# A mixture-of-experts decoder block on one core: router rows scattered without their weights, the weights sent after them in narrow scatters, the router cut into three parts

## The chip, the cores and the metric

One Trainium2 chip, one of its cores. The engines are named as in the profile: PE is TensorE (matmuls, PEld its weight loads), DVE VectorE, ACT ScalarE, POOL GpSimd, SP the SyncE queue that only issues transfers. The metric is the device time of one execution in microseconds; a kernel's time is the median of its runs.

## The reference, cut to what matters

1024 tokens (4 sequences of 256) of width 256 go through three blocks, each followed by a residual sum and a layer norm without gain: causal attention with 16 heads, a mixture in which a token's expert comes from its id, and a mixture of four experts of width 1024 with a learned router. The change touches the third block's router:

```python
logits = x @ Wr + br                       # 4 logits for each token
probs = jax.nn.softmax(logits, axis=-1)
top_w, top_idx = jax.lax.top_k(probs, 1)   # one expert, and its probability
...
h = jax.nn.silu(g) * u
y = jnp.einsum('tef,efd->ted', h, Wd)
sel = jnp.take_along_axis(y, top_idx[:, :, None], axis=1)[:, 0]
out = sel * top_w                          # then x = layernorm(x + out)
```

## The kernel before, in words

Everything is written out by hand: each engine has its own program in program order, and every dependence is a semaphore (`wait_ge`, `then_inc`). A helper `link` makes the next instruction of the same engine wait for the one before.

The **second block** leaves its rows in `XS`, 11 tiles (NS) of 128 rows; a row holds 256 values, the token's number (a large number in an empty row) and one place for the weight. It is a software pipeline of 17 rounds (`for s in range(NS + LOGIT_LAG)`, one such loop on PE, ACT and DVE). In round s tile s is transposed (L1614), tile s-1 goes through gate and product (L1155), the transposed product of tile s-2 is split into a high and a low half (L746, L1174), tile s-3 gets its residual and its statistics (L1187, L1196, L1198), tile s-4 is normalised (L1192), tile s-5 is transposed for the router (L1691, copied at L764), and tile s-6 gets its four logits (L1682). Between L1198 and L1192 POOL works out the inverse deviation of the tile (`inv_std2`, L545 and L546: add, then power).

The **router** sorts rows by expert. It runs in parts (PARTS: tiles 0 to 5, then 6 to 10). For a part DVE adds the bias, takes the largest logit and subtracts it (`logits`, L865 to L869), makes the one-hot row (`top_expert`, L877 to L883), PE counts with two matmuls how many rows of each expert stand in the same tile and ahead of a row (`count`), ACT takes the exponentials (`exps_router`), DVE forms the weight, one over their sum, and writes it into the row (`top_weight`), and DVE turns counts into a place for every row (`places`, L901 to L911). The first part's work is put into rounds 12 and 13 of DVE's loop, the second part's behind the loop. `slot_tiles` and `tile_rows` then give each of the 11 tiles of the third block its expert and its first row (L837 to L919).

POOL issues, behind the inverse deviation of the last tile, one indirect DMA for each tile that scatters its 128 rows to their places in the HBM buffer `sorted3` (L554), and then a small memset (L563) on which DVE waits before it splits three more weight chunks (L831, WINDOW). PE warms its clock with 16 matmuls of no use (`keep_warm`) when the last places are out, waits for all scatters, warms with 6 more, waits for the weight splits (`c_lo`, GATES) and transposes the first tile (L1720). SP waits for all scatters and loads the 11 tiles back in sorted order (L421).

The **third block** runs over these 11 tiles. PE does gate and up products for half a tile at a time (L1735 to L1737) and the product down (L1752 to L1754), which for tile 0 comes behind the gates of tile 2; DVE and ACT gate and split between them and also split the last weight chunks. DVE scales the result of a tile with the row's weight and adds the residual (`statistics`, L1240), POOL works out the inverse deviation, DVE normalises (L1252), and POOL scatters the rows to the output (L571).

Of the kernel before, what the change touches and what calls it, by code (L numbers as in the profile page):

```python
# [16 lines left out]
P = 128  # L17
# [33 lines left out]
PARTS = ((0, 6), (6, NS))  # L51
PART_BANK = (6, 7)
# [15 lines left out]
def build(nc, x_tok, xT, ids, wqkvT, woT, ctxT, Wr, br, Wf, out):  # L68
    ctx = ExitStack()
    with ctx:  # L70
# [24 lines left out]
        region = sb("region", [P, E], F32)  # L95
# [118 lines left out]
        sorted3 = nc.dram_tensor("sorted3", [NR3, ROW], F32, kind="Internal").ap()  # L214

# [20 lines left out]
        scat2, scat3 = sem("scat2"), sem("scat3")  # L236
# [108 lines left out]

        block = ctx.enter_context(nc.Block())
# [3 lines left out]
        def _(sp):  # L350
# [43 lines left out]
            for step in range(STEPS):  # L394
# [30 lines left out]
        def _(pool):  # L425
# [3 lines left out]
            def link(ins):  # L429
# [9 lines left out]
            g.iota(region[:, :], pattern=[[T, E]], base=0, channel_multiplier=0,  # L439
                   allow_small_or_imprecise_dtypes=True)  # L440
# [108 lines left out]
            pool.wait_ge(filled3, 16 * len(FILL_AT))  # L549
# [32 lines left out]
        def _(act):  # L582
# [127 lines left out]
            def exps_router(part):  # L710
                first, last = PARTS[part]
                act.wait_ge(lg_sb, part + 1)
                a.activation(ex[:, first:last, :], lg[:, first:last, :], ACT.Exp).then_inc(ex_rdy, 1)

            for s in range(NS + LOGIT_LAG):
# [50 lines left out]
                for part, (_, last) in enumerate(PARTS[:-1]):  # L766
                    if s == last + LOGIT_LAG:
                        exps_router(part)
            exps_router(len(PARTS) - 1)
# [50 lines left out]
        def _(dve):  # L820
# [14 lines left out]
            def slot_tiles(which, n):  # L835

                link(v.tensor_tensor(over[:, :, :], run[:, :, n - 1:n].to_broadcast([P, E, NT]),  # L837
# [20 lines left out]
            def logits(part):  # L858
# [5 lines left out]
                dve.wait_ge(id_rdy, TB)  # L864
                v.tensor_scalar(valid[:, r], XS[:, r, D], float(T), None, ALU.is_lt)  # L865
# [6 lines left out]
            def top_expert(part):  # L872
# [4 lines left out]
                link(v.tensor_scalar(ohf[:, r, :], lg[:, r, :], 0.0, None, ALU.is_ge))  # L877
# [8 lines left out]
            def top_weight(part):  # L886

                r = slice(*PARTS[part])
                dve.wait_ge(ex_rdy, part + 1)
                v.tensor_scalar(off[:, r], valid[:, r], -NOWHERE, NOWHERE, ALU.mult, ALU.add)  # L890
                link(v.reduce_sum(top[:, r], ex[:, r, :], AX.X))
                link(v.reciprocal(top[:, r], top[:, r]))
                v.tensor_scalar(XS[:, r, D + 1], top[:, r], 1 / W_SCALE, None, ALU.mult).then_inc(w_rdy, 1)

            def places(part):
# [49 lines left out]
            slot_tiles(0, NA)  # L945
# [188 lines left out]
            for s in range(NS + LOGIT_LAG):  # L1134

                for part, (_, last) in enumerate(PARTS[:-1]):
                    if s == last + LOGIT_LAG:
                        logits(part)
                        top_expert(part)
                    elif s == last + LOGIT_LAG + 1:  # L1140
                        top_weight(part)
                        places(part)
# [675 lines left out]
```

## Time and profile before

| | us |
|---|---|
| median of 3 runs | 282.25 (281.58 to 284.64) |
| the profiled execution | 283.0 |
| its span, first to last instruction | 281.2 |
| PE busy | 235.1 (84%) |
| DVE busy | 186.3 (66%) |
| ACT busy | 134.9 (48%) |
| POOL busy | 72.5 (26%) |

The mean granted clock of PE is 0.955 of full speed; in 40 slices of 7.03 us it is 9 tenths or more in all but six, four of which (6, 5, 8 and 7 tenths) follow each other from 147.6 to 175.8 us. By engine, the chain that ended last is PE for 58% of the span, DVE for 20%, ACT for 5%, POOL for 3%; a chain is followed back from the last instruction, at each step to what released it. In a timeline a line is a start, a duration, the engine, the source line, what is written and read, and in brackets how long the engine had been idle and what released it. Time counts from the first instruction.

### The profile page before, as it was taken

Reading aid. Unit: us, or ns where it says so; the run is one execution under the profiler, and the core shown is the slowest. Engines: PE = TensorE matmul, PEld = TensorE weight load, DVE = VectorE, ACT = ScalarE, POOL = GpSimd, SP = SyncE. Lnnn points to the kernel's source line nnn. Section 1 sums busy time; section 2 is a strip of 40 time slices with the busy share of each in tenths; the row PEclk is TensorE's granted clock in tenths of the full one; section 3 lists DMA queues with packets and bytes.
Section 4 is the critical chain, followed back from the end, with each engine's and each line's share of the span. In section 5 each row is a group of like instructions: output and inputs, shape, how many; then the busy total and the mean of one; then the engine's idle time right before and its main releaser. Section 6 shows DMA issues by size and latency. Waiting matters only on the chain.

```text
span 281.2 us, 7082 instructions
## 1 busy us (share of the span) xinstructions
PE 235.1 (84%) x2724; PEld 188.2 (67%) x2740; DVE 186.3 (66%) x412; ACT 134.9 (48%) x229; POOL 72.5 (26%) x143
## 2 busy tenths in 40 slices
PE   3997898978995979899995458996969999999970
PEld 3674655756764645577984224995959999999950
DVE  2888878766996566599897517885435655655550
ACT  3683666666946944565543513783213323344200
POOL 8833001000205442032222770000214212122222
PEclk9999999999999999999996587998999999999996
DMA  6800694861397755123177123400000000000000
GB/s 199 250 3 1 174 281 111 258 180 39 98 295 213 225 189 148 44 75 90 63 291 308 44 99 85 120 18 0 21 0 22 2 14 23 19 21 21 11 3 16
DMA packets 17490, 28.64 MB, mean 102 GB/s; under 512 B 2798, under 2 KB 13039, under 8 KB 17457
## 3 DMA queue, kind: packets, MB, share of 16 engines
q1 hardware_dynamic: 16016, 25.28, 30.1%
q0 software_dynamic: 1344, 2.90, 2.9%
q8 instruction: 23, 0.38, 0.6%
q14 instruction: 11, 0.08, 0.1%
q10 hardware_dynamic: 96, 0.00, 0.0%
HBM read 19.43 MB, written 9.50 MB: 103 GB/s over the span
## 4 chain that ended last, share of the span: by engine, by line
PE 58%; DVE 20%; issue 8%; ACT 5%; POOL 3%; DMA 3%; SPq 1%; POOLq 0%; DVEq 0%; ACTq 0%
PE ps L1303 8%; PE ps L1735 7%; PE ps L1736 7%; PE ps L1737 7%; PE ps L1752 4%; PE ps L1753 4%; PE ps L1754 4%; DVE arena L980 3%; DVE wf_lo L831 3%; POOL sorted L554 3%; PE ps L1404 2%; PE ps L1452 2%; PE ps L1671 2%; DMA arena<-arena 2%; DVE arena L975 2%
## 5 line engine op out<-in xcount | busy, mean ns | idle before, releaser
L1736 PE MATMUL ps<-arena,wf_hi 128*128 128x128 f16 x352 | 60.3, 218 | 0.0
L1735 PE MATMUL ps<-arena,wf_hi 128*128 128x128 f16 x352 | 60.2, 219 | 0.0
L1737 PE MATMUL ps<-arena,wf_lo 128*128 128x128 f16 x352 | 60.2, 217 | 0.0
L1736 PEld LDWEIGHTS ps<-arena,wf_hi 128*128 x352 | 34.3, 98 | 0.2
L1735 PEld LDWEIGHTS ps<-arena,wf_hi 128*128 x352 | 33.8, 96 | 0.5 <-issue 0.3
L1737 PEld LDWEIGHTS ps<-arena,wf_lo 128*128 x352 | 33.9, 96 | 0.0
L1752 PE MATMUL ps<-wf_hi,arena 128*128 x88 | 24.8, 282 | 5.9 <-DVE arena L1240 3.4
L831 DVE SCALAR_TENSOR_TENSOR wf_lo<-ring,wf_hi 128x1024 f16<-128x1024 f32 x17 | 20.6, 1219 | 11.7 <-ACT wf_hi L590 5.9
L787 ACT ACTIVATE arena<-ps 128x512 f32<-128x512 f32 x22 | 13.1, 594 | 31.5 <-PE ps L1737 31.5
L1753 PE MATMUL ps<-wf_lo,arena 128*128 x88 | 24.8, 282 | 0.0
L1754 PE MATMUL ps<-wf_hi,arena 128*128 x88 | 24.7, 281 | 0.0
L1224 DVE SCALAR_TENSOR_TENSOR arena<-ps,arena 128x512 f32<-128x512 f32 x22 | 15.2, 690 | 10.4 <-PE ps L1737 9.6
L794 ACT ACTIVATE arena<-arena 128x512 f16<-128x512 f32 x22 | 13.8, 629 | 16.6 <-DVE arena L1224 16.6
L567 POOL TENSOR_SCALAR veps<-mv 128x1 f32<-128x1 f32 x11 | 2.4, 222 | 73.2 <-DVE mv L1246 73.2
L1303 PE MATMUL ps<-xT_hi,arena 128*128 (+1 forms) x88 | 19.8, 292 | 1.7 <-DVE arena L1155 1.0
L1231 DVE TENSOR_TENSOR arena<-arena 128x512 f16<-128x512 f32 x22 | 15.2, 690 | 8.8 <-ACT arena L794 8.8
L980 DVE TENSOR_REDUCE arena<-ps 128x4 f16<-128x1024 f32 x16 | 19.6, 1223 | 0.8 <-PE ps L1404 0.7
L1309 PE MATMUL ps<-wf_hi,ones 128*128 128x512 f16 x42 | 13.0, 456 | 6.0 <-DMA sorted<-arena,pos_i 4.1
L590 ACT ACTIVATE wf_hi<-ring 128x1024 f16<-128x1024 f32 x17 | 17.7, 1054 | 0.1
L641 ACT ACTIVATE arena<-ps 128x1024 f32<-128x1024 f32 x16 | 16.6, 1036 | 0.6 <-PE ps L1436 0.2
L571 POOL DMA_INDIRECT out<-arena,out_i x11 | 12.0, 1090 | 13.9 <-DVE arena L1252 13.9
L1436 PE MATMUL ps<-arena 128*128 128x128 f16 x144 | 12.0, 219 | 3.6 <-DMA arena<-arena 3.1
(232 smaller groups left out, 567.8 us busy)
## 6 DMA issues: line engine op xcount, KB each, us to landing
ring<-Wf SPq DMA_DIRECT2D x17, 512.0 KB, 4.1
sorted<-fill SPq DMA_DIRECT2D x5, 903.0 KB, 7.4
arena<-Wf SPq DMA_DIRECT2D x7, 512.0 KB, 8.2
arena<-sorted SPq DMA_DIRECT2D x20, 129.0 KB, 2.2
sorted<-fill SPq DMA_DIRECT2D x1, 1161.0 KB, 10.0
ring<-xT SPq DMA_DIRECT2D x4, 256.0 KB, 4.8
X<-x_tok SPq DMA_DIRECT2D x1, 1024.0 KB, 7.8
ring<-ctxT SPq DMA_DIRECT2D x2, 512.0 KB, 4.0
```

Of the source, the lines that this page charges most:

```text
L590: a.activation(chunk_dst(ORDER[n], True), src, ACT.Copy, scale=W_SCALE).then_inc(c_hi, 1)
L641: a.activation(Pf[n % 2][:, 1:3], ps[:, 4:6, :], ACT.Exp, scale=DK ** -0.5).then_inc(exped, 1)
L831: v.scalar_tensor_tensor(out=chunk_dst(ORDER[n], False), in0=staged(n)[0], scalar=W_SCALE, in1=chunk_dst(ORDER[n], True), op0=ALU.mult, op ...
L980: v.tensor_reduce(dst[:, 1], ps[:, 1:3, :].rearrange("p c (a k) -> p a c k", a=G), AX.XY, ALU.max, negate=True).then_inc(maxed, 1)
L1224: v.scalar_tensor_tensor(out=hh[:, half * 512:(half + 1) * 512], in0=ps[:, 2 * half + 1, :], scalar=inv, in1=sg[:, half * 512:(half + 1) * ...
L1303: last = t.matmul(dst, xs(k), ws(k), start=(k == 0 and m == 0), stop=(k == nk - 1 and m == 2))
L1735: t.matmul(dst, hi, a_hi[p][:, k], start=k == 0, stop=False)
L1736: t.matmul(dst, hi, a_lo[p][:, k], start=False, stop=False)
L1737: last = t.matmul(dst, lo, a_hi[p][:, k], start=False, stop=k == NK - 1)
L1752: t.matmul(ps[:, 7, 0:D], hs[:, c], hi, start=c == 0, stop=False)
L1753: t.matmul(ps[:, 7, 0:D], hs[:, c], lo, start=False, stop=False)
L1754: last = t.matmul(ps[:, 7, 0:D], ls[:, c], hi, start=False, stop=c == NF - 1)
```

## The change

The router has three parts: tiles 0 to 3, 4 to 7, 8 to 10. Rows are scattered as soon as their places are known, whatever stands in their place for the weight; the row of tile 0 goes out between the inverse deviations of tiles 8 and 9. The place of a row now comes whole out of PE: `rows_of` adds, in one accumulation, the first row of the expert's region (an identity times `region16`), the counts of all tiles ahead (all-ones times their one-hots) and the rows ahead in the tile; DVE only picks with the one-hot and adds an offset. `totals` adds up all one-hots for `slot_tiles`. The exponential and the weights are formed once for all tiles, behind everything else. The weights go, after all rows, in 11 indirect DMAs of one value per row into a buffer of their own, `sorted_w` (filled with zeros at the start), and 11 loads bring them back into `w3`, which takes over the memory of `valid`. The first scaling of the third block waits for them.

```diff
-PARTS = ((0, 6), (6, NS))
-PART_BANK = (6, 7)
+PARTS = ((0, 4), (4, 8), (8, NS))
+PART_BANK = (6, 7, 6)
+TOTAL_BANK = 7
...
+                    sp.dma_start(sorted_w.rearrange("(p n) o -> p (n o)", p=P),
+                                 fill[:, 0:NR3 // P]).then_inc(filled3, 16)
...
+            rows = []
             for i in range(NS):
-                row = sp.value_load(row_i[0:1, i:i + 1], min_val=0, max_val=NR3 - P)
+                rows.append(sp.value_load(row_i[0:1, i:i + 1], min_val=0, max_val=NR3 - P))
                 if i == 0:
                     sp.wait_ge(scat3, 16 * NS)
-                sp.dma_start(XS[:, i, :], sorted3[bass.ds(row, P), :]).then_inc(ld3[i], 16)
+                sp.dma_start(XS[:, i, :], sorted3[bass.ds(rows[i], P), :]).then_inc(ld3[i], 16)
+            sp.wait_ge(scat_w, 16 * NS)
+            for i in range(NS):
+                sp.dma_start(w3[:, i:i + 1], sorted_w[bass.ds(rows[i], P), :]).then_inc(in_w, 16)
...
             def scatter3(part, i):
                 pool.wait_ge(pos_rdy, part + 1)
-                pool.wait_ge(w_rdy, part + 1)
...
-            for i in range(NS):
+            for i in range(NS - 2):
                 inv_std2(i)
+            scatter3(0, 0)
+            inv_std2(NS - 2)
+            inv_std2(NS - 1)
             for part, (first, last) in enumerate(PARTS):
-                for i in range(first, last):
+                for i in range(max(first, 1), last):
                     scatter3(part, i)
             g.memset(veps[:, :], 0.0).then_inc(scat3_sent, 1)
+            pool.wait_ge(w_rdy, 1)
+            for i in range(NS):
+                g.indirect_dma_start(sorted_w[:, :], bass.IndirectOffsetOnAxis(ap=pos_i[:, i:i + 1], axis=0),
+                                     top[:, i:i + 1], None, bounds_check=NR3 - 1,
+                                     oob_is_err=False).then_inc(scat_w, 16)
...
+            act.wait_ge(lg_sb, len(PARTS))
+            a.activation(ex[:, :, :], lg[:, :, :], ACT.Exp).then_inc(ex_rdy, 1)
...
-                link(v.tensor_scalar(ohf[:, r, :], lg[:, r, :], 0.0, None, ALU.is_ge))
+                link(v.scalar_tensor_tensor(out=ohf[:, r, :], in0=lg[:, r, :], scalar=0.0,
+                                            in1=valid[:, r].unsqueeze(2).to_broadcast([P, n, E]),
+                                            op0=ALU.is_ge, op1=ALU.mult))
...
-                link(v.scalar_tensor_tensor(out=ohf[:, r, :], in0=where[:, r, :], scalar=1.0, in1=ohf[:, r, :],
-                                            op0=ALU.is_equal, op1=ALU.mult))
-                v.tensor_tensor(oh[:, r, :], ohf[:, r, :], valid[:, r].unsqueeze(2).to_broadcast([P, n, E]),
-                                ALU.mult).then_inc(oh_rdy, 1)
...
+                v.scalar_tensor_tensor(out=oh[:, r, :], in0=where[:, r, :], scalar=1.0, in1=ohf[:, r, :],
+                                       op0=ALU.is_equal, op1=ALU.mult).then_inc(oh_rdy, 1)
+
+            def real_rows():
+                dve.wait_ge(id_rdy, TB)
+                link(v.tensor_scalar(valid[:, :], XS[:, :, D], float(T), None, ALU.is_lt))
+                link(v.tensor_scalar(off[:, :], valid[:, :], -NOWHERE, NOWHERE, ALU.mult, ALU.add))
+
+            def top_weights():
+                dve.wait_ge(ex_rdy, 1)
+                link(v.reduce_sum(top[:, :], ex[:, :, :], AX.X))
+                link(v.reciprocal(top[:, :], top[:, :]))
+                v.tensor_scalar(top[:, :], top[:, :], 1 / W_SCALE, None, ALU.mult).then_inc(w_rdy, 1)
...
-                dve.wait_ge(cnt_rdy, part + 2)
+                dve.wait_ge(place_rdy, part + 1)
                 dve.wait_ge(scat2, 16 * NA)
-                v.tensor_copy(cnt[:, :, r], ps[:, PART_BANK[part], 256:256 + n * E].rearrange("p (i e) -> p e i", e=E))
-                link(v.tensor_tensor(cum[:, r, :], ps[:, PART_BANK[part], 0:n * E].rearrange("p (i e) -> p i e", e=E),
-                                     region[:, :].unsqueeze(1).to_broadcast([P, n, E]), ALU.add))
-                running()
-                link(v.tensor_tensor(cum[:, r, :], cum[:, r, :], cnt[:, :, r].rearrange("p e i -> p i e"),
-                                     ALU.subtract))
-                link(v.tensor_tensor(where[:, r, :], cum[:, r, :],
-                                     run[:, :, r].rearrange("p e i -> p i e"), ALU.add))
-                link(v.tensor_tensor(where[:, r, :], where[:, r, :], oh[:, r, :], ALU.mult))
+                link(v.tensor_tensor(where[:, r, :], ps[:, PART_BANK[part], 256:256 + n * E].rearrange(
+                    "p (i e) -> p i e", e=E), oh[:, r, :], ALU.mult))
...
+                if s == NS + 3:
+                    logits(1)
+                    top_expert(1)
...
+                if s == NS + 1:
+                    places(0)
...
+                if s == NS - 1:
+                    real_rows()
+                    logits(0)
+                    top_expert(0)
+
+            places(1)
             last = len(PARTS) - 1
             logits(last)
             top_expert(last)
-            top_weight(last)
             places(last)
-            slot_tiles(1, NS)
+            dve.wait_ge(total_rdy, 1)
+            slot_tiles(1, ps[:, TOTAL_BANK, 384:384 + E].unsqueeze(2))
             tile_rows()
+            top_weights()
...
+                if i == 0:
+                    dve.wait_ge(in_w, 16 * NS)
                 if i >= 2:
                     dve.wait_ge(scat_out[p], 16 * (i // 2))
-                v.scalar_tensor_tensor(out=res[p], in0=ps[:, 7, 0:D], scalar=XS[:, i, D + 1:D + 2],
+                v.scalar_tensor_tensor(out=res[p], in0=ps[:, 7, 0:D], scalar=w3[:, i:i + 1],
...
+            def rows_of(part):
+
+                first, last = PARTS[part]
+                n = last - first
+                at_ = ps[:, PART_BANK[part], 256:256 + n * E].rearrange("p (i e) -> p i e", e=E)
+                pe.wait_ge(lg_sb, part + 1)
+                if part == 0:
+                    pe.wait_ge(region_rdy, 1)
+                t.matmul(at_, identH[:, :], region16[:, :].unsqueeze(1).to_broadcast([P, n, E]), start=True, stop=False)
+                for j in range(first):
+                    t.matmul(at_, ones[:, :], oh[:, j:j + 1, :].to_broadcast([P, n, E]), start=False, stop=False)
+                pe.wait_ge(oh_rdy, part + 2)
+                for j in range(first, last - 1):
+                    m = last - 1 - j
+                    t.matmul(at_[:, n - m:n, :], ones[:, :], oh[:, j:j + 1, :].to_broadcast([P, m, E]),
+                             start=False, stop=False)
+                t.matmul(at_, before[:, :], oh[:, first:last, :], start=False, stop=True).then_inc(place_rdy, 1)
+
+            def totals():
+                pe.wait_ge(pos_rdy, len(PARTS) - 1)
+                for j in range(NS):
+                    last = t.matmul(ps[:, TOTAL_BANK, 384:384 + E], ones[:, :], oh[:, j, :], start=j == 0, stop=j == NS - 1)
+                last.then_inc(total_rdy, 1)
...
+                if s == NS:
+                    rows_of(0)
+                elif s == NS + 4:
+                    rows_of(1)
+            rows_of(2)
+            totals()
```

## Rows read from the trace of the kernel before

**Rows 1.** The chain that ended last, 166 to 174 us: start, us, engine, written tile, line.

```profile
168.70 3.51 DVE wf_lo L831 x3
172.31 0.66 PE ps L1720 x2
```

**Rows 2.** Timeline of POOL, the end of the second block and the row scatters.

```profile
153.80 0.57 POOL L546 TENSOR_TENSOR rstd<-veps,minus_half 128x1 f32<-128x1 f32 x1
154.64 1.15 POOL L554 DMA_INDIRECT sorted<-arena,pos_i  x1 [0.27 <-issue]
156.09 0.97 POOL L554 DMA_INDIRECT sorted<-arena,pos_i  x1 [0.30 <-issue]
...
167.58 0.98 POOL L554 DMA_INDIRECT sorted<-arena,pos_i  x1 [0.30 <-issue]
```

**Rows 3.** Timeline of DVE, rounds 11 to 13 of the second block.

```profile
144.73 0.41 DVE L1155 SCALAR_TENSOR_TENSOR arena<-ps,arena 128x256 f32<-128x256 f32 x1
145.40 0.42 DVE L1174 TENSOR_TENSOR arena<-ps,arena 128x256 f16<-128x256 f32 x1 [0.27 <-ACT arena L746]
...
146.85 0.18 DVE L1198 BATCH_NORM_AGGREGATE mv<-st 128x2 f32<-128x6 f32 x1
146.96 0.17 DVE L865 TENSOR_SCALAR valid<-arena 128x6 f32<-128x6 f32 x1
...
148.45 0.42 DVE L1174 TENSOR_TENSOR arena<-ps,arena 128x256 f16<-128x256 f32 x1
...
149.89 0.18 DVE L1198 BATCH_NORM_AGGREGATE mv<-st 128x2 f32<-128x6 f32 x1
...
152.03 0.17 DVE L911 TENSOR_TENSOR pos_i<-pos,off 128x6 int32<-128x6 f32 x1
...
153.23 0.18 DVE L1198 BATCH_NORM_AGGREGATE mv<-st 128x2 f32<-128x6 f32 x1
```

**Rows 4.** Timeline of all engines, end of tile 0 of the third block.

```profile
200.39 0.41 DVE L1252 TENSOR_SCALAR arena<-arena,mv,rstd 128x256 f32<-128x256 f32 x1 [1.00 <-POOL rstd L569]
...
201.62 1.09 POOL L571 DMA_INDIRECT out<-arena,out_i  x1 [1.26 <-DVE arena L1252]
```

**Rows 5.** Timeline of all engines, a scatter of the attention beside a weight split.

```profile
97.68 1.54 POOL L523 DMA_INDIRECT sorted<-X,pos_i  x1 [0.30 <-issue]
...
98.30 1.22 DVE L831 SCALAR_TENSOR_TENSOR wf_lo<-ring,wf_hi 128x1024 f16<-128x1024 f32 x1
```

**Rows 6.** Timeline of PE, the last router transposes and logits, then the warming matmuls.

```profile
154.95 0.67 PE L1691 MATMUL ps<-identF,arena 128*128 128x128 f32 x2
156.09 1.01 PE L1682 MATMUL ps<-wr_sb,arena 128*128 128x4 f32 x4 [0.47 <-ACT arena L764]
...
160.86 5.02 PE L1309 MATMUL ps<-wf_hi,ones 128*128 128x512 f16 x16 [1.88 <-DVE pos_i L911]
169.96 2.20 PE L1309 MATMUL ps<-wf_hi,ones 128*128 128x512 f16 x6 [4.08 <-DMA sorted<-arena,pos_i]
```

**Rows 7.** Busy time by stretch; behind the engines the granted clock, DMA share, GB/s.

```profile
171.00:172.00 1.00, 1.00 (x3) 0.15 (x1) 1.00 (x2) 0.00 (x0) 0.00 (x0) 0.50 0.49 132
```

**Rows 8.** The page's DMA issues: KB each, then median us from issue to landing.

```profile
arena<-sorted SPq DMA_DIRECT2D x20, 129.0 KB, 2.2
...
sorted<-arena,pos_i POOLq DMA_INDIRECT x11, 2.7
```

**Rows 9.** Timeline of SP: the queue's issues.

```profile
34.05 0.43 SPq L364 DMA_DIRECT2D sorted<-fill  x1
...
141.49 3.42 SPq L381 DMA_DIRECT2D arena<-Wf  x7
170.10 11.75 SPq L421 DMA_DIRECT2D arena<-sorted  x11
```

**Rows 10.** Timeline of DVE, third block: the first scaling with a weight.

```profile
198.16 0.48 DVE L1240 SCALAR_TENSOR_TENSOR arena<-ps,arena 128x256 f32<-128x256 f32 x1 [4.07 <-PE ps L1754]
```

**Rows 11.** Timeline of ACT, behind the router's second exponential.

```profile
158.08 1.28 ACT L770 ACT_TABLE_LOAD   x1
```

More of the change, by code:

```diff
@@ L94, in build @@
         steps = sb("steps", [P, NS], F32)
-        region = sb("region", [P, E], F32)
+        region16 = sb("region16", [P, E], F16)
         tiles = sb("tiles", [P, NS], F32)
@@ L214, in build @@
         sorted3 = nc.dram_tensor("sorted3", [NR3, ROW], F32, kind="Internal").ap()
+        sorted_w = nc.dram_tensor("sorted_w", [NR3, 1], F32, kind="Internal").ap()
         in_ids, in_wo, in_xtok, in_r = (sem(n) for n in ("in_ids", "in_wo", "in_xtok", "in_r"))
@@ L235, in build @@
         oh_rdy, cnt_rdy, cnt_sb, pos_rdy, tile_rdy = (sem(n) for n in ("oh_rdy", "cnt_rdy", "cnt_sb", "pos_rdy", "tile_rdy"))
-        scat2, scat3 = sem("scat2"), sem("scat3")
+        place_rdy, total_rdy, region_rdy = sem("place_rdy"), sem("total_rdy"), sem("region_rdy")
+        scat2, scat3, scat_w, in_w = sem("scat2"), sem("scat3"), sem("scat_w"), sem("in_w")
         scat_out = [sem(f"scat_out{i}") for i in range(2)]
@@ L344, in rows_in @@
             return 64 * (b + 1) - 32
+        w3 = valid
         block = ctx.enter_context(nc.Block())
@@ L438, in _ @@
                    allow_small_or_imprecise_dtypes=True)
-            g.iota(region[:, :], pattern=[[T, E]], base=0, channel_multiplier=0,
-                   allow_small_or_imprecise_dtypes=True)
+            g.iota(region16[:, :], pattern=[[T, E]], base=0, channel_multiplier=0,
+                   allow_small_or_imprecise_dtypes=True).then_inc(region_rdy, 1)
             g.memset(cnt[:, :, :], 0.0)
@@ L547, in inv_std2 @@
                                 ALU.pow).then_inc(rs2, 1)
-            pool.wait_ge(filled3, 16 * len(FILL_AT))
+            pool.wait_ge(filled3, 16 * (len(FILL_AT) + 1))
             def scatter3(part, i):
                 pool.wait_ge(pos_rdy, part + 1)
-                pool.wait_ge(w_rdy, part + 1)
                 g.indirect_dma_start(sorted3[:, :], bass.IndirectOffsetOnAxis(ap=pos_i[:, i:i + 1], axis=0),
@@ L708, in _ @@
             a.activation(sg_s[:, 0:1], identF[:, 0:1], ACT.Silu)
[L710 to L713, printed above, removed]
             for s in range(NS + LOGIT_LAG):
@@ L765, in _ @@
                                  ACT.Copy).then_inc(x2T_sb, 1)
[L766 to L769, printed above, removed]
+            act.wait_ge(lg_sb, len(PARTS))
+            a.activation(ex[:, :, :], lg[:, :, :], ACT.Exp).then_inc(ex_rdy, 1)
             a.activation(sg[:, 0:1], identF[:, 0:1], ACT.Silu)
@@ L833, in split_lo, with slot_tiles @@
                                        op1=ALU.subtract).then_inc(c_lo, 1)
-            def slot_tiles(which, n):
-                link(v.tensor_tensor(over[:, :, :], run[:, :, n - 1:n].to_broadcast([P, E, NT]),
+            def slot_tiles(which, totals):
+                link(v.tensor_tensor(over[:, :, :], totals.to_broadcast([P, E, NT]),
                                      steps[:, 0:NT].unsqueeze(1).to_broadcast([P, E, NT]), ALU.is_gt))
@@ L863, in logits @@
                 dve.wait_ge(in_r, 32)
-                dve.wait_ge(id_rdy, TB)
-                v.tensor_scalar(valid[:, r], XS[:, r, D], float(T), None, ALU.is_lt)
                 link(v.tensor_tensor(lg[:, r, :], ps[:, PART_BANK[part], 0:n * E].rearrange("p (i e) -> p i e", e=E),
@@ L880, in top_expert @@
                                           ohf[:, r, :].rearrange("p i e -> p (i e)"), 0.0, ALU.mult, ALU.add))
-                link(v.scalar_tensor_tensor(out=ohf[:, r, :], in0=where[:, r, :], scalar=1.0, in1=ohf[:, r, :],
-                                            op0=ALU.is_equal, op1=ALU.mult))
-                v.tensor_tensor(oh[:, r, :], ohf[:, r, :], valid[:, r].unsqueeze(2).to_broadcast([P, n, E]),
-                                ALU.mult).then_inc(oh_rdy, 1)
[L886 to L893, printed above, removed]
+                v.scalar_tensor_tensor(out=oh[:, r, :], in0=where[:, r, :], scalar=1.0, in1=ohf[:, r, :],
[9 more added lines that the diff above has]
+                v.tensor_scalar(top[:, :], top[:, :], 1 / W_SCALE, None, ALU.mult).then_inc(w_rdy, 1)
             def places(part):
@@ L944, in _ @@
             running()
-            slot_tiles(0, NA)
+            slot_tiles(0, run[:, :, NA - 1:NA])
             def proj_lo(tt):
@@ L1134, in _ @@
             for s in range(NS + LOGIT_LAG):
[L1136 to L1142, printed above, removed]
+                if s == NS + 3:
+                    logits(1)
+                    top_expert(1)
                 if s < NS:
@@ L1680, in _ @@
                     bank, col = PART_BANK[part], i - PARTS[part][0]
+                    if col == 0 and part >= 2:
+                        pe.wait_ge(pos_rdy, part - 1)
                     for k in range(NK):
@@ L1692, in _ @@
                     last.then_inc(x2T_rdy, 1)
-                for part, (first, last) in enumerate(PARTS[:-1]):
-                    if s == last + LOGIT_LAG:
-                        pe.wait_ge(oh_rdy, part + 2)
-                        count(PART_BANK[part], first, last)
-            pe.wait_ge(oh_rdy, len(PARTS) + 1)
-            count(PART_BANK[-1], *PARTS[-1])
+                if s == NS:
[4 more added lines that the diff above has]
+            totals()
             def expert_of(i):
```

## The prediction

> **What bounds the kernel now.** I read the engine shares and the row of granted clocks on the page first, then the chain that ended last, then the timelines of the engines around the router. TensorE is on the chain for most of the span, but nothing in the change touches the attention or the size of the expert matmuls. The part it touches runs from the end of the second block (145 us) to the first expert matmul (174 us), and there the chain hangs on three things in a row [rows 1]: GpSimd's scatters, VectorE's three weight splits that may start only when the last scatter is written out (3.51 us), and TensorE's first transpose at 172.31.
>
> The eleven scatters run back to back: the first starts at 154.64, the last at 167.58, and from the second on they are (167.58 - 156.09) / 9 = 1.277 us apart [rows 2]. They start when GpSimd has finished the last inverse deviation, at 153.80 + 0.57 = 154.37. The places of the first six tiles had been there since 152.03 + 0.17 = 152.2 [rows 3], so the chain is "last inverse deviation, then eleven times 1.277". Removing the wait for the weights alone gives nothing, since the places were always the later of the two. What can be won is (a) scatters taken out of the row of eleven, and (b) an earlier last inverse deviation, which hangs on VectorE's row of instructions.
>
> **(1) VectorE, first part moved ahead.** Before: eight small instructions from 146.96 to 148.45 (1.49 us) and twelve from 149.99 to 152.12 (2.13 us) [rows 3]. Now eight stand at the end of round 10, all but the last linked, about 0.21 us each: 1.61 us, from 144.73 on. The gate product, first in round 11, slides from 144.73 to 146.34, the next low split from 145.40 to 146.67 (+1.27). TensorE's last transpose of h and the product behind it hang on that split, so the low split of the last sorted tile, 148.45 before with the old block in front of it, comes at about 148.77. TensorE itself waits about 0.9 us for the one-hots in round 11; nobody else needs it then.
>
> **(2) places(0)** is three instructions (0.6 us) instead of twelve: 149.1 to 149.7. The statistics of tile 9, at 149.89 before, come at 150.72.
>
> **(3) The scatter moved ahead.** The statistics of tile 8, 146.85 before, come at 148.12, and GpSimd needs 154.37 - (153.23 + 0.18) = 0.96 us behind such statistics [rows 2, 3]; it has done inverse deviation 8 by 149.3 and waits for the places at 149.7. From a release to the start of an indirect DMA the trace shows 201.62 - (200.39 + 0.41) = 0.82 us [rows 4], and 1.09 for the scatter itself. It runs from 150.5 to about 151.6. Inverse deviation 9, which could have begun at 150.9, stands behind it and ends at 152.5; VectorE's normalisation of tile 9 waits for it, and the statistics of tile 10 stand behind that: about 153.3, against 153.23 before. So what VectorE saves (1.49 + 2.13 - 1.61 - 0.6 = 1.4 us) is spent on waiting for GpSimd: **(b) is worth nothing**, bounded by +0.6 (the scatter starts at once and delays nothing) and -0.9 (clock low in round 12, or a scatter of 1.54 us as in [rows 5]).
>
> **(4) Ten scatters behind it instead of eleven: -1.28 us.** Condition: places in time. Scatter 4 goes out at about 158.7, so part 1 has to be placed by 157.9. The last transpose, 154.95 before, comes at 155.1 [rows 6]; nine small matmuls follow. They are not in this trace; by nothing at all below and by a fourth of the four logit matmuls' 1.01 us above, they cost 0 to 2.3 us. I take 1.0 (half precision, low clock), then 0.7 for three VectorE instructions and a semaphore: 157.5. Margin 0.4; at the upper end scatter 4 and all behind it are 0.9 late. Part 2 is ready at 160.3 and needed at 163, so the eleven matmuls of the totals and the tile rows lie under the scatters. The 16 warming matmuls start at about 160.7, near their 160.86 of before [rows 6].
>
> **(5) Behind the scatters.** Splits and row loads shift with the last scatter. Ahead of them TensorE idled 4.08 us [rows 6], and a microsecond after that the granted clock was 0.50, the 1.2 GHz level [rows 7]; the first transpose then took 0.66 [rows 1]. The idle time shrinks to about 3.0 us; if the clock stays at 2.4 GHz, half of the 0.66 comes back. Against it, narrow scatters now run beside the first row load, which lands 2.2 us after its issue [rows 8], level with the end of the splits: 0 to 1 us late, I take 0.1. The two cancel at half a chance for the clock.
>
> **(6) Narrow scatters and loads.** Eleven more scatters on GpSimd, which had nothing to do between the row scatters and the end of tile 0, and eleven more loads on SP, which was done at 170.10 + 11.75 = 181.9 [rows 9]. They start at about 167.6. With VectorE busy a scatter took up to 1.54 [rows 5]; I take 1.09 + 0.30 apart: 15.3 us, to 183, landed (2.7 [rows 8]) by 185.6. SP then issues eleven loads whose registers it already holds: by its seven weight loads 3.42 / 7 = 0.49 each, by the row loads with their register reads 11.75 / 11 = 1.07. With 0.49: 191, landed at 193.2. The first reader is the scaling of tile 0, at 198.16 before [rows 10], now 196.9. So it is hidden, with 3.7 us to spare. Cover gone, VectorE would stop at that line, with the gates of tile 3 queued behind it.
>
> **(7) Hidden.** The fill of the weight buffer is one more issue of 0.43 us [rows 9] at the first attention step, where SP's next load waits for a split. The single exponential moves behind the last logits (158.5): two table loads of 1.28 [rows 11], two activations and three splits, done by 164.5, with VectorE asking for them at 167.5. VectorE's weights end at 164, and GpSimd wants them at 167.5.
>
> **A rule weighed.** VectorE's split with both inputs in SBUF took 1.22 us beside a scatter that itself was stretched to 1.54 [rows 5]: GpSimd yielded, VectorE did not. The Trainium skill ("SBUF — State Buffer", on the port pair that VectorE and GpSimd share) says that whichever starts first holds the pair for the whole instruction and the other blocks fully. By the row the splits at 168 lose nothing; by the rule each could stand behind a narrow scatter, rival C.
>
> **Sum.** -1.28 (4), 0 (b), 0 (5): -1.3 us. The profiled execution took 283.0 (span 281.2 and 1.8 around it), which becomes 281.7; it lies 0.75 above the median of the runs, 282.25, which becomes **281.0**.
>
> **Rivals.**
> A, *the moved scatter eats itself* (chance 0.20): the detour of (3) pushes the last inverse deviation back by more than I worked out, or scatter 4 waits for its places. For it: only 0.4 us of margin in both. Against: the old row had 3.6 us of VectorE work in the same place. Cost 0.9 to 1.3: 281.9 to 282.4. This is also the case in which the change does not do what it says.
> B, *more comes back* (0.15): the scatter delays nothing (0.6) and the clock holds (0.3 to 0.6, the warming matmuls in front of the first experts included): 279.8 to 280.1.
> C, *GpSimd gets in VectorE's way* (0.05): each of the three splits waits for one scatter of up to 0.97 us: +2.9 - 1.3, so 283.9. Against it stands the split of 1.22 us [rows 5].
> D, *the weights come late* (0.08), the slower side: scatters 1.84 apart (1.54 + 0.30) and loads 1.07 apart give 167.6 + 20.2 + 2.7 + 11.8 + 2.2 = 204.5, where 196.9 is wanted. That is 7.6 late and up to 288.6; it decides from the point at which the 3.7 us are used up, and 4.1 us past it the time is over 1% worse.
> My forecast has 0.52.
>
> **Numbers.** 1% is about what a measurement of this kernel can tell from no change: 279.4 to 285.1. Nothing above reaches below 279.4 except B with both its bounds and the runs' own spread; I give that 0.08. Slower by over 1% is most of D: 0.08. The range takes in forecast, A and B, with 0.6 us of spread at either side: 279.3 to 283.2.
>
> **What would show it.** Right: one scatter between the inverse deviations 8 and 9 at about 150.5, ten in a row from about 154.7, VectorE's three splits at 167.5 and 1.2 us each, the first transpose at 171. Wrong: the statistics of tile 10 later than 153.5 (A), a gap ahead of the fifth scatter (A), VectorE idle before the first scaling with the narrow loads as releaser (D), or splits longer or apart (C).

## The result, and the profile after

The changed kernel is **slower**: 289.01 us median (287.3 to 291.54) against 282.05, a ratio of 1.0246 (95% interval 1.0186 to 1.0306). The profiled execution took 289.97 (span 288.2). The forecast was 281.0.

A fixed point for both traces is GpSimd's add of tile 7, the last thing that the change leaves alone. In the kernel before, from GpSimd's timeline (start, us, engine, line, operation), it and the memset behind the last row scatter:

```profile
144.90 0.22 POOL L545 TENSOR_SCALAR veps<-mv 128x1 f32<-128x1 f32 x1 [1.64 <-DVE mv L1198]
...
168.53 0.14 POOL L563 MEMSET veps<- 128x2 f32 x1
```

The same view of the kernel after, answering to [rows 2]:

```profile
143.92 0.26 POOL L556 TENSOR_SCALAR veps<-mv 128x1 f32<-128x1 f32 x1 [1.64 <-DVE mv L1200]
...
149.44 1.09 POOL L564 DMA_INDIRECT sorted<-arena,pos_i  x1 [1.25 <-DVE pos_i L915]
150.57 0.24 POOL L556 TENSOR_SCALAR veps<-mv 128x1 f32<-128x1 f32 x1
...
152.86 0.57 POOL L557 TENSOR_TENSOR rstd<-veps,minus_half 128x1 f32<-128x1 f32 x1
153.60 1.09 POOL L564 DMA_INDIRECT sorted<-arena,pos_i  x1 [0.18 <-issue]
...
165.20 0.97 POOL L564 DMA_INDIRECT sorted<-arena,pos_i  x1 [0.30 <-issue]
166.17 0.12 POOL L576 MEMSET veps<- 128x2 f32 x1
166.48 1.91 POOL L579 DMA_INDIRECT sorted_w<-top,pos_i  x1 [0.19 <-issue]
168.69 1.97 POOL L579 DMA_INDIRECT sorted_w<-top,pos_i  x1 [0.30 <-issue]
...
184.09 0.97 POOL L579 DMA_INDIRECT sorted_w<-top,pos_i  x1 [0.30 <-issue]
```

Up to the memset 168.53 - 144.90 = 23.63 us became 166.17 - 143.92 = 22.25: 1.38 won, with one scatter between two inverse deviations and ten in a row. From the memset to the end of the span 281.2 - 168.53 = 112.67 became 288.2 - 166.17 = 122.03: **9.36 lost**. TensorE's timeline in the expert matmuls shows most of it. The bracket is the idle time ahead of the instruction and its releaser; "issue" means that the engine waited for nothing that the profile shows:

```profile
183.26 0.22 PE L1773 MATMUL ps<-arena,wf_lo 128*128 128x128 f16 x1 [0.81 <-issue]
184.23 0.22 PE L1771 MATMUL ps<-arena,wf_hi 128*128 128x128 f16 x1 [0.75 <-issue]
184.87 0.22 PE L1772 MATMUL ps<-arena,wf_hi 128*128 128x128 f16 x1 [0.43 <-issue]
190.82 0.29 PE L1773 MATMUL ps<-arena,wf_lo 128*128 128x128 f16 x1 [3.30 <-issue]
```

That is 5.29 us of standing still in the middle of gate products. Before, the same matmuls have no such gap. These are all of TensorE's waits from 174 to 200 us there (engine, tile and line, releaser: us in total, times, longest); the one wait is for the last weight split, ahead of the first down product:

```profile
PE ps L1752 <- DVE wf_lo L831: 2.4, 1, 2.4
```

In the kernel after, the granted clock is at its lower level, 1.2 GHz, behind the longest of the four stops (busy time by stretch; behind the engines the clock, the DMA engines' share, GB/s). The last line is the stretch with the highest DMA share from 168 to 200 us:

```profile
190.00:192.00 2.00, 1.18 (x11) 1.14 (x12) 0.00 (x0) 0.00 (x0) 0.00 (x0) 0.50 0.34 105
192.00:194.00 2.00, 2.00 (x20) 1.94 (x18) 1.06 (x2) 0.79 (x2) 0.00 (x0) 0.50 0.09 8
...
176.00:178.00 2.00, 2.00 (x39) 2.00 (x37) 1.90 (x3) 2.00 (x4) 1.70 (x2) 1.00 1.31 39
```

From the first gate matmul to the first down product it is 199.69 - 171.62 = 28.07 us, where the kernel before needs 193.67 - 174.22 = 19.45. The gaps make 5.29 of these 8.62. The low clock makes most of the rest: from 190.82 to 196.7 the matmuls run at half speed, which gives away some 2.9 us (an estimate).

The DMA share adds up the whole time of each packet that starts in the stretch, so it can pass 1. The packets of those 2 us took 1.31 times the time that 16 engines have, while only 39 GB/s were moved. The same view of the kernel before, at a like place, has 0.53 and 131 GB/s:

```profile
178.00:180.00 2.00, 2.00 (x39) 2.00 (x37) 1.50 (x3) 2.00 (x4) 0.00 (x0) 1.00 0.53 131
```

SP's timeline and the DMA issues (KB each, median us to landing) show who suffers, beside [rows 8] and [rows 9]:

```profile
167.72 16.79 SPq L429 DMA_DIRECT2D arena<-sorted  x11
195.62 5.35 SPq L432 DMA_DIRECT2D valid<-sorted_w  x11
```

```profile
arena<-sorted SPq DMA_DIRECT2D x11, 129.0 KB, 8.2
```

The row loads land 8.2 us after their issue instead of 2.2, and SP, which must wait for the narrow scatters, begins the narrow loads at 195.62. What TensorE waits for shows in the DMA queues (queue: packets, MB, share of 16 engines' time in the stretch). In 186.5 to 187 us of the kernel after, one packet of instructions starts:

```profile
q8 instruction: 1, 0.02, 42.1%
```

The packet's whole time counts where it starts: 0.421 x 16 x 0.5 = 3.37 us. In the kernel before, 188 to 192 us holds one such packet:

```profile
q8 instruction: 1, 0.02, 1.4%
```

That is 0.014 x 16 x 4 = 0.90 us. TensorE stops at 187.52 and goes on at 190.82, some 0.8 us after this packet is through (186.6 + 3.37). That q8 carries TensorE's program can be read from its pace. In the kernel before, from 178 us on, a packet starts after every 212 to 281 recorded instructions of TensorE (matmuls, weight loads and waits), at first at 178.00, 183.58 and 189.74. In the kernel after no packet starts between 172.93 and 186.61; 417 instructions go by, and the three shorter stops (1.99 us together) fall into the end of that stretch. So packets start late and then take long: **the small writes hold up the reading of TensorE's own program.** That the stops are waits for instructions is inferred from this coincidence, since the profile names no releaser for them. The packet at 172.93 took 2.84 us and no stop came with it, so a long packet alone does not stop TensorE.

### The profile page after: what moved, and what is told of

Same layout as the page of the kernel before. It is cut to its first block, busy times and chain, and to the rows that moved or that the text cites. A ratio compares the mean times of both kernels' runs of the same rounds, so it can differ in the third digit from the quotient of the medians.

```text
span 288.2 us, 7189 instructions
## 1 busy us (share of the span) xinstructions
PE 239.5 (83%) x2757; PEld 192.0 (67%) x2773; DVE 186.3 (65%) x404; ACT 134.9 (47%) x228; POOL 88.1 (31%) x154
## 4 chain that ended last, share of the span: by engine, by line
PE 59%; DVE 18%; issue 10%; ACT 6%; DMA 3%; POOL 2%; SPq 0%; POOLq 0%; ACTq 0%; DVEq 0%
PE ps L1337 8%; PE ps L1771 7%; PE ps L1773 7%; PE ps L1772 7%; PE ps L1788 4%; PE ps L1789 4%; PE ps L1790 4%; DVE arena L984 2%; PE ps L1438 2%; PE ps L1486 2%; PE ps L1705 2%; DVE wf_lo L842 2%; DVE arena L958 2%; ACT wf_hi L608 1%; DVE arena L979 1%
## 5 line engine op out<-in xcount | busy, mean ns | idle before, releaser
L1773 PE MATMUL ps<-arena,wf_lo 128*128 128x128 f16 x352 | 62.8, 222 | 4.1 <-issue 4.1
L1771 PE MATMUL ps<-arena,wf_hi 128*128 128x128 f16 x352 | 62.8, 223 | 1.1 <-issue 0.8
L1772 PE MATMUL ps<-arena,wf_hi 128*128 128x128 f16 x352 | 62.8, 222 | 0.4 <-issue 0.4
L1773 PEld LDWEIGHTS ps<-arena,wf_lo 128*128 x352 | 34.9, 99 | 3.7 <-issue 3.7
L1771 PEld LDWEIGHTS ps<-arena,wf_hi 128*128 x352 | 34.6, 98 | 2.4 <-issue 2.2
L1772 PEld LDWEIGHTS ps<-arena,wf_hi 128*128 x352 | 35.2, 100 | 1.1 <-issue 0.9
L1232 DVE SCALAR_TENSOR_TENSOR arena<-ps,arena 128x512 f32<-128x512 f32 x22 | 15.2, 691 | 18.1 <-PE ps L1773 9.5
L579 POOL DMA_INDIRECT sorted_w<-top,pos_i x11 | 15.5, 1413 | 3.2 <-issue 3.2
L1343 PE MATMUL ps<-wf_hi,ones 128*128 128x512 f16 x42 | 12.3, 438 | 3.9 <-DMA sorted<-arena,pos_i 3.5
```

What stands on the lines that cost most here:

```text
L579: g.indirect_dma_start(sorted_w[:, :], bass.IndirectOffsetOnAxis(ap=pos_i[:, i:i + 1], axis=0), top[:, i:i + 1], None, bounds_check=NR3 - ...
L1771: t.matmul(dst, hi, a_hi[p][:, k], start=k == 0, stop=False)
L1772: t.matmul(dst, hi, a_lo[p][:, k], start=False, stop=False)
L1773: last = t.matmul(dst, lo, a_hi[p][:, k], start=False, stop=k == NK - 1)
```

## The experiments

In all of them "up to the memset" is the time from the add of tile 7 to the memset behind the last row scatter, "behind it" the rest of the span, both from the profiled execution; the ratio is to the kernel before.

**The change without its narrow scatters.**

```
-            pool.wait_ge(w_rdy, 1)
-            for i in range(NS): g.indirect_dma_start(sorted_w ...)
-            sp.wait_ge(scat_w, 16 * NS)
-            for i in range(NS): sp.dma_start(w3[:, i:i + 1], ...)
-                       scalar=w3[:, i:i + 1],
+                       scalar=XS[:, i, D + 1:D + 2],
```

> The changed kernel without its eleven narrow scatters, without the eleven narrow loads and without the wait for them (the weights are left out: every row of the third block is scaled with the zero that stands in it). Theory T1: the narrow scatters fill the DMA engines from 166 to 195 us, the row loads land 8 us after their issue and TensorE, in the middle of its expert matmuls, waits for its own instructions. Then all of the loss goes with them: row loads land in about 2.1 us again, TensorE has no idle time put down to issue among the gate matmuls, and the time is 280.5 to 281.5 us, 1 us or so under the kernel before. Theory T2: the added instructions of TensorE and their place in its program are what makes it wait, whatever the transfers do: the idle times at 182 to 196 us stay and the time is 286 to 289. In both the chain up to the first transpose should be that of the changed kernel, since nothing there is touched.

The scaling then takes the zero that lies in the row, so the experts' products drop out of the sum. Measured: 282.51 us, ratio 1.0029 (0.9979 to 1.0079), so T2 falls, though the 1 us under the kernel before that T1 expected is not seen. Up to the memset 22.26, behind it 112.55. The 9.4 us are gone, no gate matmul waits on issue, and the row loads land in 2.1. What the change does to order and placement of the code alone costs nothing of this size.

**The kernel before, with eleven narrow scatters that nobody reads.**

```
             g.memset(veps[:, :], 0.0).then_inc(scat3_sent, 1)
+            pool.wait_ge(w_rdy, len(PARTS))
+            for i in range(NS):
+                g.indirect_dma_start(sorted_w[:, :], ... pos_i ..., top[:, i:i + 1] ...)
```

> The kernel before, with nothing added but the eleven narrow scatters behind the row scatters, into a buffer that nobody reads and that nobody waits for until the end. Theory T1: the loss moves over with them: 286 to 290 us, TensorE idle on issue somewhere between 180 and 200 us, row loads landing at 5 to 12 us. Theory T2: 282 to 283, as the kernel before, since TensorE's program is unchanged to the last instruction.

Measured: 293.4 us, ratio 1.0381 (1.0302 to 1.0459); behind the memset 121.75. TensorE's waits (engine, line, releaser: us in total, times, longest):

```profile
PE ps L1742 <- issue: 4.5, 3, 2.2
```

The writes alone do it; the narrow loads are not needed. The loss is larger than T1 expected, and the row loads (landing in 3.9) suffer less. Here 485 instructions of TensorE go by between the q8 packets at 177.81 and 195.77, and all its stops on issue but the last (2.17 us, up to 198.12) fall into that stretch; a packet's record may be missing there.

**The change with its weights 128 bytes apart.** As many scatters, as many 4-byte writes, the same loads; only the addresses differ.

```
-        sorted_w = nc.dram_tensor("sorted_w", [NR3, 1], ...)
+        sorted_w = nc.dram_tensor("sorted_w", [NR3 * PITCH, 1], ...)
+        w_rows = sorted_w.rearrange("(r c) o -> r (c o)", c=PITCH)   # PITCH = 32
-   ... ap=pos_i[:, i:i + 1] ...
+   ... ap=pos_w[:, i:i + 1] ...                                      # pos_w = pos * PITCH
```

> The changed kernel with its weight buffer stretched: each weight stands 128 bytes from the next instead of 4, with the same number of 4-byte writes and reads, and two small VectorE instructions more for the indices. Theory T3, a narrower T1: it is not small writes as such that are slow but many of them into the same few stretches of memory, since neighbours in the buffer are written by the same scatter. Then narrow scatters land in 3 to 4 us, the row loads in 2 to 3, and the time falls to 281 to 283. If small writes as such fill the engines, nothing changes: 287 to 290. The filling at the start grows from 17.5 to 573 KB and should cost nothing.

Measured: 282.98 us, ratio 1.0002 (0.996 to 1.0043); behind the memset 113.53. The narrow scatters still run beside the expert matmuls, 0.97 to 2.03 us each, and DMA is at ease. This is its busiest stretch from 168 to 186 us:

```profile
178.00:180.00 2.00, 2.00 (x40) 2.00 (x38) 2.00 (x4) 1.45 (x3) 1.70 (x2) 1.00 0.53 123
```

So neither the number of scatters nor the 4 bytes of a write matter, but that writes are **neighbours**. The kernel without any narrow scatter has 1.0029, so at this distance they cost nothing that can be measured. The Trainium skill ("DMA: Bandwidth & Descriptors", Specifications) says that a transfer under 512 B is done by read-modify-write. By that alone the writes 128 bytes apart should cost as much as the dense ones. They cost nothing measurable, and the measurement decides.

**32 bytes apart, 8 bytes apart.** The kernel above with PITCH = 8 and PITCH = 2.

> The kernel after with the weights 32 bytes apart in DRAM instead of 4 (128 bytes apart cost nothing: ratio 1.0002). Same number of narrow scatters and loads. T3a, the writes disturb each other when they fall into one stretch larger than 32 bytes: row loads land late again (over 5 us at the median), TensorE idles on issue in the gates, ratio 1.01 to 1.025. T3b, only writes into the same 32 bytes do: row loads land in about 2.4 us, ratio 0.996 to 1.004 like the kernel with 128 bytes.

Measured: 282.81 us, ratio 1.0027 (0.9989 to 1.0065); behind the memset 112.87, no gate waits on issue, row loads landing in 2.7. 32 bytes suffice.

> The kernel after with the weights 8 bytes apart instead of 4 (32 and 128 bytes apart cost nothing: ratios 1.0027 and 1.0002). T4a, the writes disturb each other because several fall into one stretch of up to 32 bytes: row loads land late (5 us or more at the median), TensorE idles on issue in the gates, ratio 1.01 to 1.025. T4b, only writes next to each other without a gap do: row loads land in about 2.4 us, ratio 0.998 to 1.005.

Measured: 303.54 us, ratio 1.0711 (1.0642 to 1.078). This is far more than either theory said, and most of it lies elsewhere: the add of tile 7 comes at 164.06, 20 us late, before any narrow scatter has started. Behind the memset it is 116.81, 4.1 over the kernel before. For that part T4a holds: the row loads land in 5.4 us, TensorE stops once on issue in the gates (1.88 us, up to 207.28), and 4.1 us are 1.5%. The culprit of the 20 us is the fill of the buffer at the first attention step, which this edit also cuts into 8-byte pieces. The DMA issues of the stretch 34 to 66 us in the kernel with 8 bytes:

```profile
arena<-arena SPq DMA_DIRECT2D x4, 2.0 KB, 14.8
sorted_w<-fill SPq DMA_DIRECT2D x1, 35.0 KB, 31.1
```

and with 32 bytes, where four times as much is written:

```profile
sorted_w<-fill SPq DMA_DIRECT2D x1, 140.0 KB, 12.2
arena<-arena SPq DMA_DIRECT2D x4, 2.0 KB, 2.4
```

One such fill makes the 2 KB transfers that the attention waits for take 14.8 us at the median instead of 2.4, and TensorE then waits for it (18.1 us at once). No GpSimd is in this: a plain transfer from SP's queue, cut into small neighbouring writes, does the same. Between 8 and 32 bytes lies the limit; nothing in between was tried. The Trainium skill has the nearest rule in "Collectives: The Full Stack" (Rules for kernel authors): buffers aligned to 32 bytes avoid a read-modify-write. The traces agree with its 32 bytes, for ordinary transfers; whether a read-modify-write is what costs here, no run shows.

**Four narrow scatters instead of eleven,** in the kernel before.

> The kernel before plus four of the eleven narrow scatters that nobody reads (eleven cost a ratio of 1.0381, 10.7 us). Theory L, that each costs about the same: +3.5 to 4.3 us, ratio 1.012 to 1.016. Rival, that only those that run beside the expert matmuls' first code and the row loads' packets count and four are over by then, or that a backlog has to build up first: ratio 0.998 to 1.006.

Measured: 287.77 us, ratio 1.0222 (1.0153 to 1.0292), but the four executions took 281.51, 287.63, 287.91 and 291.51. The profiled one is the 281.51. Its row loads suffered (4.2 us to landing, 15.84 us of issuing on SP), yet TensorE has no gap on issue and behind the memset it is 112.31. Late row loads cost nothing in it. Its q8 packet at 175.34 took 4.87 us, the longest in these experiments behind the memset, and TensorE did not stop either: a slow packet need not cost anything. What made the other three longer is not shown. No trace of them was kept, and beside them the kernel before itself took up to 286.73. A race between the writes and a packet of instructions would fit, but that is argued, and neither theory is settled by this run.

**Eleven narrow scatters, but late.** In the kernel before, they wait until the ninth row load has landed.

```
+            pool.wait_ge(w_rdy, len(PARTS))
+            pool.wait_ge(ld3[8], 16)
+            for i in range(NS): g.indirect_dma_start(sorted_w ...)
```

> The kernel before plus the eleven narrow scatters that nobody reads (ratio 1.0381 when they run from 168.8 on), now held back until the ninth row load has landed, so from about 181 to 196.5, while GpSimd has nothing else to do before 199.5. The row loads are then out of their way and land in 2.0 to 2.5 us. Theory R, that late row loads are what costs: ratio 0.998 to 1.004. Theory F, that the narrow writes hold up the fetch of TensorE's own instructions, whatever is loaded: TensorE idles on issue in the gate or down matmuls behind 181, in gaps of 0.5 us and more that sum to over 3 us, and the ratio is 1.015 to 1.04.

Measured: 287.37 us, ratio 1.0212 (1.0161 to 1.0263); behind the memset 117.88. The row loads land in 2.1 us as ever, so theory R falls. TensorE's timeline, and the queues in 202.5 to 203 us:

```profile
204.63 0.22 PE L1745 MATMUL ps<-arena,wf_lo 128*128 128x128 f16 x1 [0.80 <-issue]
...
205.98 0.22 PE L1744 MATMUL ps<-arena,wf_hi 128*128 128x128 f16 x1 [0.99 <-issue]
```

```profile
q8 instruction: 1, 0.02, 38.9%
```

The packet of instructions takes 0.389 x 16 x 0.5 = 3.11 us, from 202.8 to 205.9; TensorE stops twice in that time and goes on for good at 205.98. Theory F holds in kind. Its size was expected at over 3 us of gaps; here there are 1.8, and then 6.8 us at the lower clock (207.2 to 214.1). If half of those are given away (an estimate), 1.8 + 3.4 make the 5.2 us lost behind the memset. A packet at 188.78 that took 2.80 us stopped nothing.

**The early scatter by itself.** The first experiment with all eleven scatters behind the last inverse deviation.

```
-            for i in range(NS - 2): inv_std2(i)
-            scatter3(0, 0)
-            inv_std2(NS - 2); inv_std2(NS - 1)
+            for i in range(NS): inv_std2(i)
```

> The kernel after without narrow scatters and loads (they scale with the zero in the row, as in the first experiment), and without the scatter between the inverse deviations: eleven in a row behind the last of them. From tile 7's first add on GpSimd to the memset behind the last row scatter: 22.26 us with the early scatter, 23.63 in the kernel before. By the working of the prediction, that the early scatter takes one from the row (-1.28) and the earlier deviation is worth nothing: 23.5 to 23.6. Rival, from the trace with the early scatter, where the add of tile 9 ran 0.76 us behind its statistics: the last deviation comes 0.76 us earlier without it, and the row has eleven again (+1.28): 22.8 to 22.9. Ratio of the time 1.00 to 1.006 either way.

Measured: 282.9 us, ratio 1.0006 (0.9972 to 1.004). Up to the memset, 167.17 - 144.30:

```profile
144.30 0.25 POOL L553 TENSOR_SCALAR veps<-mv 128x1 f32<-128x1 f32 x1 [1.64 <-DVE mv L1189]
...
167.17 0.13 POOL L570 MEMSET veps<- 128x2 f32 x1
```

22.87, as the rival said. The lighter VectorE row alone is worth 23.63 - 22.87 = 0.76, nearly all of it by an earlier last deviation (its add comes 7.93 us behind the add of tile 7, before 8.60), and the early scatter adds 22.87 - 22.26 = 0.61.

**Weights left in the rows.** Three parts, TensorE's count and the early scatter, with the exponential and the weights done per part as before; no narrow scatters.

```
+                pool.wait_ge(w_rdy, part + 1)           # in scatter3
+                v.tensor_scalar(XS[:, r, D + 1], top[:, r], 1 / W_SCALE, ...)
```

> A version that keeps what worked of the change (three parts, TensorE counting the places, the first row scatter moved ahead) and puts the weights back into the rows before these are scattered: the exponential in three parts, its table loaded in round 11 where ScalarE has time, and three small VectorE instructions per part, put where VectorE waits anyway. No narrow transfer is left. T1 and T3: 280.5 to 281.5 us, 0.3 to 0.5% under the kernel before. T2: 286 to 289, as with the changed kernel.

Measured: 281.61 us, ratio 0.9998 (0.9968 to 1.0027). T2 falls, but the 0.3 to 0.5% are not seen. Up to the memset 23.17 (0.46 won), since the early scatter starts 6.24 us behind the add of tile 7 instead of 5.52. That is one execution: with the ten matmuls below, the same program up to there took 22.44. Behind the memset 110.63, the shortest of all, and for another reason: every other trace has pieces of about 3.4 us at the lower clock behind the memset, this one none before 275.

**Is the clock what hides the 1.4 us?** TensorE idles 2.4 us ahead of the first down product, for the last weight split, and the clock falls there. Ten matmuls of 512 columns that nobody reads go into that gap, in the kernel before, in the one with weights in the rows, and in the one with 128 bytes:

```
                 if i == 2:
+                    keep_warm(10, wf_hi[:, 0:512], bank=4)
                     down(0, bases[0])
```

> The kernel before, with ten matmuls of 512 columns (2.1 us at the full clock, into a bank nobody reads) ahead of the first down product, where TensorE idles 2.4 us for the last weight split and the granted clock falls to 0.50 behind it. Theory K, that the clock behind this wait hides what the router gives: the clock stays 1.00 through the first down product, which gets 1.5 to 2 us shorter, ratio 0.993 to 0.995. Rival, that the clock falls there for another reason or that the expert matmuls behind it wait for something else anyway: 0.998 to 1.002.

> Weights kept in the rows, three parts, TensorE counts the places, early scatter (0.46 us gained up to the last scatter), plus the same ten matmuls ahead of the first down product. Theory K: ratio to the kernel before 0.991 to 0.994, which is 0.4 to 0.5 us under the kernel before with the ten matmuls. Rival: 0.998 to 1.001 as without them.

> The kernel after with the weights 128 bytes apart (1.4 us gained up to the last row scatter) plus the same ten matmuls. Theory K: ratio 0.987 to 0.990, some 1.4 us under the kernel before with the ten matmuls. Rival, that the 1.4 us are lost behind the router whatever the clock: equal to the kernel before with the ten matmuls, within 0.4 us.

Measured: ratios 1.0014 (0.9979 to 1.005), 0.9992 (0.9961 to 1.0022) and 1.0046 (1.0015 to 1.0076). The gap is filled and the clock holds there, but it falls elsewhere. The kernel before at 195 us:

```profile
195.00:196.00 1.00, 1.00 (x7) 0.69 (x6) 0.00 (x0) 0.00 (x0) 0.00 (x0) 0.50 0.00 0
```

and the same with the ten matmuls:

```profile
195.00:196.00 1.00, 1.00 (x11) 0.90 (x10) 0.00 (x0) 0.00 (x0) 0.00 (x0) 1.00 0.00 0
208.00:209.00 1.00, 1.00 (x6) 0.71 (x5) 0.07 (x1) 0.00 (x0) 0.79 (x2) 0.50 0.00 0
```

Behind the memset it takes 112.66 as against 112.67. With 128 bytes the low clock stays longer at 168 to 174 instead (113.01). Theory K falls: filling this gap is not the lever. None of these kernels is measurably faster than the kernel before.

## Why the prediction was wrong, step by step

- **(1) to (4)**: the sum was right, 1.38 won against 1.28 + 0. The split between its two terms was not, so it is luck that it came out. The trace after shows the scatter at 149.44, the deviation behind it at 150.57 and VectorE idle for 1.37 us, just as worked out, but without the early scatter the last deviation would have come 0.7 earlier. So moving one scatter ahead is worth 0.61, not 1.28, and the lighter row 0.76, not nothing. Part 1 was placed at 155.5, two us before the fifth scatter (157.55); rival A did not occur.
- **(5)**: the first transpose came at 170.06, 3.89 us behind the memset where it was 172.31 - 168.53 = 3.78. It waited 1.01 for the row load, as foreseen in kind, and the clock was at 2.4 GHz in return (transposes of 0.41 instead of [rows 1]'s 0.66).
- **(6) is the step that failed.** "So it is hidden, with 3.7 us to spare" took the narrow scatters for row scatters with less in them, and the sum holds nothing for them; 9.36 us were lost behind the memset. Spacing was (184.09 - 166.48) / 10 = 1.76 us, not 1.39, but that is not what hurt: it is 1.79 with the weights 128 bytes apart, where SP begins the narrow loads at 187.86 and nothing is lost. With dense writes the last landing came 195.62 - 185.06 = 10.6 us after the last scatter ended, not 2.7. Above all, the step asked only who reads the weights, not what else uses the DMA engines meanwhile: the row loads (8.2 us to landing) and TensorE's own instructions (3.37 us a packet instead of 0.90).
- **Rival D** came close in time (288.6) by the wrong mechanism. The weights were late against the 196.9 that the old schedule wanted, but VectorE never waited for them. It reached the first scaling at 204.19, released by TensorE, where [rows 10] had 198.16:

```profile
204.19 0.48 DVE L1250 SCALAR_TENSOR_TENSOR arena<-ps,valid,arena 128x256 f32<-128x256 f32 x1 [4.07 <-PE ps L1790]
```

- **Rival C** fell, and the rule weighed with it. Beside scatters stretched to 1.91 and 1.97 us the three splits took what they took in [rows 1]:

```profile
166.32 3.50 DVE L842 SCALAR_TENSOR_TENSOR wf_lo<-ring,wf_hi 128x1024 f16<-128x1024 f32 x3 [5.25 <-POOL veps L576]
```

  By the lock of the Trainium skill's "SBUF — State Buffer", which goes to whichever starts first, the first scatter, waiting since 166.48, should have had its turn ahead of the second split. No split waited; GpSimd alone paid.
- **(7)**: the fill of the dense buffer is hidden (landing 9.8 us, nobody late), but only because each partition writes its 140 bytes (17.5 KB over 128) in one piece; twice as much, cut into 8-byte pieces, costs 20 us.
- **The gain of 1.4 us itself** was not seen in the time. The four kernels that have it up to the memset and no dense writes gave 1.0029, 1.0002, 1.0027 and, with the ten matmuls, 1.0046, where 0.995 would answer to it; 0.995 lies below all four intervals. Single executions differ by more: GpSimd's second product on an operand loaded from DRAM starts at 19.35 to 22.51 us in the fourteen traces, which are the same up to there, and, in the traces without dense writes, the time behind the memset varies from 110.6 to 114.4 with the length of the pieces at the lower clock. Which of these takes back the gain, or what else does, stays open.

## What to carry to other kernels

Before calling a transfer hidden, ask what its writes do to everyone else on the DMA engines, the engines' own instruction packets included, and not only who reads it. Give scattered scalars a stretch of at least 32 bytes each: eleven scatters of 128 such values cost 7 to 11 us next to each other and nothing measurable (ratio 0.9989 to 1.0065) at a pitch of 32. When an engine idles on "issue" in the middle of straight code, look at the instruction queue's packets and at the DMA engines' load.

## What was not expected of the hardware

- Small neighbouring writes fill the DMA engines' time (a share of 1.31 at 39 GB/s) with little bandwidth used, and slow unrelated transfers: row loads 2.2 to 8.2 us, a 2 KB transfer 2.4 to 14.8, a 16 KB instruction packet 0.90 to 3.37.
- Behind the memset no packet of q8 took over 1.41 us in the nine traces without dense writes; with them the longest took 2.21 to 4.87, but for 1.50 in the kernel before with eleven. A slow packet need not cost anything: beside the one of 4.87 us, with four narrow scatters, TensorE did not stop.
- A filled gap doesn't buy the clock back: the piece at 1.2 GHz moved from 194.4 to 207.4 us and the time stayed.
